# Graph-network kernel: the gather streams wait one group further back, and each gets a limit on how far it runs ahead

## The chip, the cores and the metric

One core of a Trainium2 chip runs the whole program. The metric is the device time of one execution in microseconds (us); less is better. TensorE, VectorE (DVE), ScalarE (ACT) and GpSimd (POOL) compute; SyncE (SP) and POOL's own queue start transfers. A row gather or row scatter is an indirect DMA and is started by GpSimd.

## The reference, cut to what matters

100,000 nodes with 16 features, 50,000 edges (`src`, `dst`, an 8-way type, a 90-way type, a weight, 16 attributes). Four graph layers follow each other, each on `h = relu(layernorm(x))` and added back to `x`:

```python
x = x + L0(h)   # two graph attention layers (3 heads x 32, then 1 x 32), SELU, linear
x = x + L1(h)   # two relational convolutions, 8 relations, mean over edges of one relation
x = x + L2(h)   # msg = w * xi * xj / (5 + 0.9*xi + 0.1*xj), summed at the source node
x = x + L3(h)   # per-edge 16x16 matrix out of 90, times an attention scalar, summed at dst
```

Each layer needs `table[src[e]]` for every edge e, a sum (or a softmax) over the edges of one destination, and then dense work per node.

## The kernel before, in words

The edges are first sorted by destination. Slot (p, s) holds one edge, p a partition and s a column, with T = 392 columns. An edge's source row lies in an HBM table, so one column of 128 edges is one indirect DMA from GpSimd (a "gather"): `ring[:, s]` receives the 128 rows. A "stream" is the loop over the 392 columns in one stage. Between the stages stands a barrier of all engines and every stage has its own semaphores.

The stages in order, with the line of their gather or scatter:

- setup, counting and sorting (gather L521, scatter L809), then a stage in which 56 columns of the first attention stream are gathered (L984);
- **attention 1**: columns 56 to 391 (L1147). DVE takes them in 9 chunks of 48: `edge_score(i)` (first instruction L1271) waits until its columns have landed, `edge_sum(i)` and `edge_mix(i)` (last instruction L1362, semaphore `mix_ok`) follow. Between them dense work goes on (3 blocks for a chunk);
- **attention 2**: 392 columns (L1487), chunks of 40: `edge_score(i)` starts at L1617, `edge_sum(i)` raises `ring_free` at L1637. The ring holds 200 columns;
- **relational 1**: 392 columns (L1817); `expand` (L2010, semaphore `expand_ok`) takes 8 columns at a time, 49 times, and TensorE and ScalarE work on its result;
- **relational 2**: 392 columns (L2128), a ring of 240; TensorE transposes 4 columns at a time (L2160, `lift_ok`), DVE reduces the product (L2240, L2243) and then raises `taken`, 98 times;
- **source sums**: gathers (L2338) alternating with accumulating scatters (L2352); the pacing function serves only its first 80 gathers;
- a dense stage, in which GpSimd has nothing to do;
- **last layer**: 392 gathers (L2573); DVE takes 8 columns at a time: `choose` (L2643), then L2655 to L2665, `mats_used` after L2660. On the same GpSimd queue, behind the last gather, 393 scatters of the finished rows (L2583) follow, paced by `spaced`, which always waits for the group two back. One plain copy to the output ends the kernel.

GpSimd runs its queue in order. `paced` stands ahead of every gather of the five named streams. At each eighth column it waits until an earlier group of eight has wholly landed: below column 160 (`RUN`) the group two back, so that up to 16 gathers may be under way, and from column 160 on the group just started, so that GpSimd waits until nothing of its own is under way (a "drain" below). A full ring is kept from being overwritten by one `hold` per 40 columns (`hold` is a plain semaphore wait). In attention 1 and the last layer the ring has all 392 columns and there is no such wait.

Of the kernel before, what the change touches and what calls it, by code (L numbers as in the profile page):

```python
# [49 lines left out]
def hold(engine, sem, value):  # L50

    engine.wait_ge(sem, value)


BATCH = 8


RUN = 160


def paced(engine, landing, s, first=0):

    n = s // BATCH - (1 if s >= RUN else 2)
    if s % BATCH == 0 and n >= first // BATCH:
        engine.wait_ge(landing[n], 16 * BATCH)


def spaced(engine, landing, s):  # L70


    n = s // BATCH - 2
    if n >= 0:
        engine.wait_ge(landing[n], 16 * BATCH)


def all_landed(engine, landing, lo, hi):

    for n in range(lo // BATCH, -(-hi // BATCH)):  # L80
        engine.wait_ge(landing[n], 16 * (min(hi, BATCH * (n + 1)) - BATCH * n))
# [6 lines left out]
def gnn_kernel(nc, x, src, dst, edge_attr_16, edge_type_8, edge_type_90, edge_weight,  # L88
# [45 lines left out]
    with ExitStack() as top:  # L134
# [43 lines left out]
        with ExitStack() as ctx:  # L178
            def tmp(name, shape, dt=F32):
                return sb(name, shape, dt, ctx)  # L180

            def sem(name):
                return semaphore(ctx, name)
# [753 lines left out]
        with ExitStack() as ctx:  # L937
# [29 lines left out]
            with nc.Block() as block:  # L967
# [9 lines left out]
                @block.gpsimd  # L977
                def _(pool):
                    nc.gpsimd.iota(trash[:], pattern=[[1, T + 1]], base=NP, channel_multiplier=T + 1,
                                   allow_small_or_imprecise_dtypes=True).then_inc(trash_ok, 1)  # L980
                    hold(pool, src_ok, 1)
                    for s in range(EARLY):
                        paced(pool, gat_in, s)
                        pool.indirect_dma_start(ring1[:, s, :], None, t_gat1,  # L984
                                                bass.IndirectOffsetOnAxis(src_i[:, s:s + 1], 0)
                                                ).then_inc(gat_in[s // BATCH], 16)
                    all_landed(pool, gat_in, 0, EARLY)
# [101 lines left out]
        with ExitStack() as ctx:  # L1089
# [3 lines left out]
            def sem(name):  # L1093
# [3 lines left out]
            NE, EW = 9, 48  # L1097
# [27 lines left out]
            step_s, arg_ok, exp_e, mix_ok, tail_ok, bm_ok, reach_ok, at_ok, att_ok, ext_ok = (sem(n) for n in (  # L1125
                "step", "arg", "exp_e", "mix", "tail", "bm", "reach", "at", "att", "ext"))
# [15 lines left out]
            with nc.Block() as block:  # L1142
                @block.gpsimd
                def _(pool):
                    for s in range(EARLY, T):
                        paced(pool, gat_in, s, EARLY)
                        pool.indirect_dma_start(ring1[:, s, :], None, t_gat1,  # L1147
                                                bass.IndirectOffsetOnAxis(src_i[:, s:s + 1], 0)
                                                ).then_inc(gat_in[s // BATCH], 16)
                    all_landed(pool, gat_in, EARLY, T)  # L1150
# [255 lines left out]
        QN = 40  # L1406
# [14 lines left out]
        with ExitStack() as ctx:  # L1421
# [3 lines left out]
            def sem(name):  # L1425
# [3 lines left out]
            NR = 5  # L1429
# [3 lines left out]
            lead = tmp("lead", [P, 1])  # L1433
# [26 lines left out]
            mix_ok, elu_ok, ready_ok, flip_ok, copy_ok, prod_ok, var_ok, root_ok, row_ok = (  # L1460
                sem(n) for n in ("mix", "elu", "ready", "flip", "copy", "prod", "var", "root", "row"))
            x_in = [sem(f"x_in{k}") for k in range(4)]
            ring_free, const_ok = sem("ring_free"), sem("const")
# [16 lines left out]
            with nc.Block() as block:  # L1480
                @block.gpsimd
                def _(pool):
                    for s in range(T):
                        if s % QN == 0 and s >= NR * QN:
                            hold(pool, ring_free, s // QN - NR + 1)
                        paced(pool, gat_in, s)
                        pool.indirect_dma_start(ring[:, s % (NR * QN), :], None, t_gat2,  # L1487
                                                bass.IndirectOffsetOnAxis(idx2[:, s:s + 1], 0)
                                                ).then_inc(gat_in[s // BATCH], 16)
                    all_landed(pool, gat_in, 0, T)  # L1490
# [271 lines left out]
        def relation_pass(tag, table, table_out, F, CW, weights, root, bias, NR, norm, setup):  # L1762

            EXPAND = NREL * F // P
            ES = 8
            BS = 4 // EXPAND
            NB = ES // BS
            subs = [w // ES for w in widths]
            first = [sum(subs[:i]) for i in range(NE)]
            sub_at = {}  # L1770
            for i in range(NE):
                for s in range(subs[i]):
                    n = 3 * i - 1 + (s + 1) // 2
                    sub_at.setdefault(max(n, 0), []).append((i, s))
            PROD = 1024 if CW * QN > 1024 else 1536
            with ExitStack() as ctx:
# [3 lines left out]
                def sem(name):  # L1780
                    return semaphore(ctx, f"{tag}_{name}")
# [21 lines left out]
                step_s, expand_ok, lift_ok, drop_ok, turn_ok, y_in, sum_ok, tail_ok, ext_ok = (  # L1803
                    sem(n) for n in ("step", "expand", "lift", "drop", "turn", "y_in", "sum", "tail", "ext"))
# [4 lines left out]
                with nc.Block() as block:  # L1809
                    @block.gpsimd  # L1810
                    def _(pool):
                        for s in range(T):
                            if s % QN == 0 and s >= NR * QN:
                                i = s // QN - NR
                                hold(pool, expand_ok, first[i] + subs[i])
                            paced(pool, gat_in, s)
                            pool.indirect_dma_start(ring[:, s % (NR * QN), :], None, table,  # L1817
                                                    bass.IndirectOffsetOnAxis(idx2[:, s:s + 1], 0)
                                                    ).then_inc(gat_in[s // BATCH], 16)
                        all_landed(pool, gat_in, 0, T)  # L1820
# [265 lines left out]
        with ExitStack() as ctx:  # L2086
# [6 lines left out]
            F, CW, NR = CH, FEAT, 6  # L2093
            ES = 4
            subs = [w // ES for w in widths]
            first = [sum(subs[:i]) for i in range(NE)]
            sub_at = {}
            for i in range(NE):
# [17 lines left out]
            step_s, lift_ok, drop_ok, product_ok, taken, tail_ok, ext_ok = (  # L2116
                sem(n) for n in ("step", "lift", "drop", "product", "taken", "tail", "ext"))
            flip_ok, copy_ok, prod_ok, used_ok, var_ok, root_ok, row_ok = (
                sem(n) for n in ("flip", "copy", "prod", "used", "var", "root", "row"))
            with nc.Block() as block:  # L2120
                @block.gpsimd
                def _(pool):
                    for s in range(T):
                        if s % QN == 0 and s >= NR * QN:
                            i = s // QN - NR
                            hold(pool, lift_ok, first[i] + subs[i])
                        paced(pool, gat_in, s)
                        pool.indirect_dma_start(ring[:, s % (NR * QN), :], None, t_rel2,  # L2128
                                                bass.IndirectOffsetOnAxis(idx2[:, s:s + 1], 0)
                                                ).then_inc(gat_in[s // BATCH], 16)  # L2130
                    all_landed(pool, gat_in, 0, T)
# [164 lines left out]
        ES = 8  # L2296
# [4 lines left out]
        with ExitStack() as ctx:  # L2301
# [10 lines left out]
            lead = tmp("lead", [P, FEAT])  # L2312
# [226 lines left out]
        with ExitStack() as ctx:  # L2539
# [3 lines left out]
            def sem(name):  # L2543
                return semaphore(ctx, f"l3_{name}")

            subs = [w // ES for w in widths]
            first = [sum(subs[:i]) for i in range(NE)]
# [3 lines left out]
            lead = tmp("lead", [P, 1])  # L2551
# [12 lines left out]
            lead_ok, lead_in, pick_ok, mats_ok, mats_used, tail_ok, ext_ok, final_ok, step_s = (sem(n) for n in (  # L2564
                "lead", "lead_in", "pick", "mats", "mats_used", "tail", "ext", "final", "step"))
            dense_out, copied = sem("dense_out"), sem("copied")
            sent = [sem(f"sent{n}") for n in range(T // BATCH + 1)]
            with nc.Block() as block:  # L2568
                @block.gpsimd
                def _(pool):  # L2570
                    for s in range(T):
                        paced(pool, gat_in, s)
                        pool.indirect_dma_start(ring[:, s, :], None, t_last,  # L2573
                                                bass.IndirectOffsetOnAxis(idx2[:, s:s + 1], 0)
                                                ).then_inc(gat_in[s // BATCH], 16)
                    pool.wait_ge(dense_out, 16)
                    for s in range(T + 1):
                        if s % QN == 0 and s < T:
                            hold(pool, final_ok, s // QN + 1)
                        if s == T:  # L2580
                            hold(pool, final_ok, NE + 1)
                        spaced(pool, sent, s)
                        pool.indirect_dma_start(fin, bass.IndirectOffsetOnAxis(home_i[:, s:s + 1], 0),  # L2583
                                                X[:, s, :], None).then_inc(sent[s // BATCH], 16)
                    all_landed(pool, sent, 0, T + 1)
                    all_landed(pool, gat_in, 0, T)
# [120 lines left out]
```

## Time and profile before

| | |
|---|---|
| time, median of 3 runs | 6640.55 us (6635.97 to 6644.13) |
| profiled execution: span, first to last instruction | 6645.3 us |
| GpSimd busy | 4320.0 us (65%) |
| DVE busy | 3659.5 us (55%) |
| TensorE busy | 2965.9 us (45%) |
| ScalarE busy | 1167.0 us (18%) |
| granted TensorE clock, mean | 0.654 of full |
| HBM traffic | 53 GB/s over the span |

No engine is busy throughout. The stages have different limits, so the shares say little; what counts is, within a stage, which wait ends last. The time of an indirect DMA on POOL is the time in which GpSimd prepares it, not the transfer. The idle time "<-issue" is the short pause between two POOL instructions in which nothing is waited for; "<-DMA" is a wait for a transfer, "<-POOLq L132" the wait at the barrier between two stages.

### The profile page before, as it was taken

To read this page: it belongs to the slowest core of one execution; us is meant where nothing else is said; L and a number is where in the kernel's file an instruction comes from. 1 tells how busy PE (TensorE), PEld (TensorE's weight loads), DVE (VectorE), ACT (ScalarE), POOL (GpSimd) and SP (SyncE) were. 2 spreads that over 40 slices of the span, in tenths; PEclk is the share of its full clock that TensorE was granted. 3 is DMA by queue.
4 is the path that set the end of the run, shared out by engine and by line. 5 is a ranking of instruction groups with operands and counts; after the bars stand their busy time and mean duration, and the time that the engine had idled before them with its cause. 6 is when DMAs were issued, how large, how long until landed. Compare 5 with 4: busy or idle time off the path is not lost. (4 is left out here: it accounts for less than half of the span.)

```text
span 6645.3 us, 44822 instructions
## 1 busy us (share of the span) xinstructions
PE 2965.9 (45%) x13056; PEld 2260.1 (34%) x13056; DVE 3659.5 (55%) x8917; ACT 1167.0 (18%) x1912; POOL 4320.0 (65%) x3949
## 2 busy tenths in 40 slices
PE   5798699974444344447655443111111002544000
PEld 2477555543333233346644333111111001433000
DVE  8855499976555566654347667433322068876000
ACT  0265454532222233211111100000000000000000
POOL 4666555557762776376657665888888823766776
PEclk9899899985666555556667665555555555776555
DMA  2122222221110322123222212222222234211001
GB/s 41 22 62 70 56 67 67 66 66 12 20 17 14 89 60 65 47 64 100 84 87 60 64 53 72 52 36 36 44 27 27 5 96 154 57 50 37 7 7 44
DMA packets 283354, 350.11 MB, mean 53 GB/s; under 512 B 133518, under 2 KB 204432, under 8 KB 281970
## 3 DMA queue, kind: packets, MB, share of 16 engines
q1 hardware_dynamic: 112158, 295.24, 13.2%
q0 software_dynamic: 169376, 41.40, 7.8%
q10 hardware_dynamic: 1576, 10.60, 0.7%
q8 instruction: 105, 1.72, 0.1%
q14 instruction: 139, 1.14, 0.1%
HBM read 231.06 MB, written 122.29 MB: 53 GB/s over the span
## 5 line engine op out<-in xcount | busy, mean ns | idle before, releaser
L2352 POOL DMA_INDIRECT acc<-l_rows,l_uniq x392 | 624.1, 1592 | 121.0 <-issue 108.6
L2573 POOL DMA_INDIRECT l_ring<-t_last,idx x392 | 392.4, 1001 | 366.5 <-ACTq L2568 207.6
L521 POOL DMA_INDIRECT pay<-in_x,gidx x392 | 460.1, 1174 | 235.4 <-DMA pay<-in_x,gidx 114.3
L2393 PE MATMUL ps_l<-l_msg,l_alike 128*128 128x16 f32 x784 | 176.3, 376 | 962.4 <-DVE l_msg L2456 962.4
L1487 POOL DMA_INDIRECT g_ring<-t_gat,idx x392 | 416.1, 1062 | 278.7 <-issue 110.1
L1817 POOL DMA_INDIRECT r_ring<-t_rel,idx x392 | 414.6, 1058 | 254.6 <-issue 110.3
L809 POOL DMA_INDIRECT t_sort<-pay,c_pos x392 | 384.8, 982 | 296.3 <-DVE c_pos L875 196.3
L901 PE MATMUL ps_c<-plane,c_hit 128*128 128x400 f32 x1568 | 542.6, 499 | 1.2 <-ACT c_hit L827 1.2
L2128 POOL DMA_INDIRECT r_ring<-t_rel,idx x392 | 392.7, 1002 | 224.4 <-issue 110.4
L2338 POOL DMA_INDIRECT l_ring<-t_mix,idx x392 | 426.3, 1087 | 154.6 <-issue 119.1
L2393 PEld LDWEIGHTS ps_l<-l_msg,l_alike 128*128 128x128 f32 x784 | 171.0, 331 | 967.7 <-DVE l_msg L2456 967.7
L1147 POOL DMA_INDIRECT ring<-t_gat,src_i x336 | 368.5, 1097 | 151.5 <-issue 93.3
L2583 POOL DMA_INDIRECT fin<-X,home_i x393 | 376.9, 959 | 119.8 <-issue 119.8
L2614 PE MATMUL ps_l<-w_rel,l_pick 128*128 128x256 f32 x784 | 275.7, 528 | 272.7 <-DVE l_pick L2643 272.7
L901 PEld LDWEIGHTS ps_c<-plane,c_hit 128*128 128x128 f32 x1568 | 296.4, 190 | 208.3 <-ACT c_hit L827 1.6
L2614 PEld LDWEIGHTS ps_l<-w_rel,l_pick 128*128 128x128 f32 x784 | 212.0, 277 | 336.1 <-DVE l_pick L2643 291.6
L2451 DVE TENSOR_SCALAR l_den<-l_ring 128x128 f32<-128x128 f32 x49 | 11.2, 228 | 564.3 <-DMA l_ring<-t_mix,idx 564.3
L871 DVE SCALAR_TENSOR_TENSOR c_junk<-iota_lo,lo_f,ps_c 128x400 f32<-128x400 f16 x392 | 231.0, 623 | 63.1 <-PE ps_c L901 63.0
L688 PE MATMUL ps_a<-w_ext,a_act_t 96*128 96x128 f32 x1600 | 224.5, 286 | 40.4 <-DVE a_row L612 39.9
L688 PEld LDWEIGHTS ps_a<-w_ext,a_act_t 96*128 96x128 f32 x1600 | 214.8, 200 | 61.7 <-DVE a_row L612 49.8
L1520 PE MATMUL ps_g<-ident,g_ex 128*128 128x128 f32 x300 | 71.9, 426 | 327.0 <-DVE g_ex L1704 327.0
L622 DVE SCALAR_TENSOR_TENSOR a_act_t<-a_ex,a_pos 96x512 f32<-96x512 f32 x200 | 137.4, 687 | 143.5 <-ACT a_ex L729 140.1
(529 smaller groups left out, 8145.0 us busy)
## 6 DMA issues: line engine op xcount, KB each, us to landing
c_rows_d<-row_dst SPq DMA_DIRECT2D x98, 256.0 KB, 3.3
l_keys<-row_at SPq DMA_DIRECT2D x49, 512.0 KB, 4.2
l_typs<-row_typ SPq DMA_DIRECT2D x49, 512.0 KB, 3.7
g_hs<-t_gat SPq DMA_DIRECT2D x30, 660.0 KB, 4.7
acc<-r_zero SPq DMA_DIRECT2D x60, 320.0 KB
t_rel<-r_row SPq DMA_DIRECT2D x30, 640.0 KB, 3.5
r_hs<-t_rel SPq DMA_DIRECT2D x30, 640.0 KB, 4.7
d_gain<-acc SPq DMA_DIRECT2D x30, 640.0 KB, 6.0
```

Source lines behind the costliest of these rows:

```text
L521: pool.indirect_dma_start(pay[:, s, 8:PAY], None, x, bass.IndirectOffsetOnAxis(gidx[:, s:s + 1], 0)).then_inc(gat_in[s // BATCH], 16)
L688: last = mm(ps[:, at:at + WIDE], act_t[:, u, P * m:P * (m + 1)], w2_ext[:], start=True, stop=True, skip_group_check=True)
L809: pool.indirect_dma_start(t_sort, bass.IndirectOffsetOnAxis(pos[:, e:e + 1], 0), pay[:, e, :], None).then_inc(sent, 16)
L901: last = mm(ps[:, bank:bank + LO], hit[:, b, j, P * s:P * (s + 1)], plane[:, b, LO * j:LO * (j + 1)], start=(j == 0), stop=(j == 1))
L1487: pool.indirect_dma_start(ring[:, s % (NR * QN), :], None, t_gat2, bass.IndirectOffsetOnAxis(idx2[:, s:s + 1], 0)).then_inc(gat_in[s // BA ...
L1817: pool.indirect_dma_start(ring[:, s % (NR * QN), :], None, table, bass.IndirectOffsetOnAxis(idx2[:, s:s + 1], 0)).then_inc(gat_in[s // BAT ...
L2128: pool.indirect_dma_start(ring[:, s % (NR * QN), :], None, t_rel2, bass.IndirectOffsetOnAxis(idx2[:, s:s + 1], 0)).then_inc(gat_in[s // BA ...
L2338: pool.indirect_dma_start(ring[:, s, :], None, t_mix, bass.IndirectOffsetOnAxis(idx2[:, s:s + 1], 0)).then_inc(gat_in[s // BATCH], 16)
L2352: pool.indirect_dma_start(acc[r], bass.IndirectOffsetOnAxis(uniq[:, s:s + 1], 0), rows[:, (s // ES) % RR, s % ES, :], None, compute_op=ALU.add
L2573: pool.indirect_dma_start(ring[:, s, :], None, t_last, bass.IndirectOffsetOnAxis(idx2[:, s:s + 1], 0)).then_inc(gat_in[s // BATCH], 16)
L2583: pool.indirect_dma_start(fin, bass.IndirectOffsetOnAxis(home_i[:, s:s + 1], 0), X[:, s, :], None).then_inc(sent[s // BATCH], 16)
L2614: last = mm(ps[:, at:at + 256], pick[:, e % 2, s], w_rel[:].rearrange("p i o -> p (i o)"), start=True, stop=True)
```

## The change

It has two parts. `paced` loses its special case: at every eighth column, over the whole stream, it waits for the group two back (the gathers 9 to 16 back). And a new wait, `credit`, is put ahead of it in the five streams: at every eighth column beyond `lead`, the consumer's semaphore must have reached (s - lead) / per, rounded up, so that no column more than `lead` beyond those used is asked for (and the seven behind it). The lead is 96 columns in attention 1, 64 in attention 2 and relational 1, 32 in relational 2, 40 in the last layer. It replaces the three ring holds. In the diff the middle stream of `relation_pass` is relational 1. The stage that starts the first 56 columns and the 80 early gathers of the source sums call `paced` only below column 160.

```diff
-RUN = 160
 def paced(engine, landing, s, first=0):
-    n = s // BATCH - (1 if s >= RUN else 2)
+    n = s // BATCH - 2
     if s % BATCH == 0 and n >= first // BATCH:
         engine.wait_ge(landing[n], 16 * BATCH)
+def credit(engine, used, s, lead, per):
+    if s % BATCH == 0 and s > lead:
+        engine.wait_ge(used, -(-(s - lead) // per))
@@ attention 1
                     for s in range(EARLY, T):
+                        credit(pool, mix_ok, s, 2 * EW, EW)
                         paced(pool, gat_in, s, EARLY)
@@ attention 2
-                        if s % QN == 0 and s >= NR * QN:
-                            hold(pool, ring_free, s // QN - NR + 1)
+                        credit(pool, ring_free, s, 64, QN)
                         paced(pool, gat_in, s)
@@ relational 1
-                            if s % QN == 0 and s >= NR * QN:
-                                i = s // QN - NR
-                                hold(pool, expand_ok, first[i] + subs[i])
+                            credit(pool, expand_ok, s, 64, ES)
                             paced(pool, gat_in, s)
@@ relational 2
-                        if s % QN == 0 and s >= NR * QN:
-                            i = s // QN - NR
-                            hold(pool, lift_ok, first[i] + subs[i])
+                        credit(pool, taken, s, 32, ES)
                         paced(pool, gat_in, s)
@@ last layer
                     for s in range(T):
+                        credit(pool, mats_used, s, 40, ES)
                         paced(pool, gat_in, s)
```

## Rows read from the trace of the kernel before

**Rows 1.** Page, costliest groups: the scatters that end the kernel.

```profile
L2583 POOL DMA_INDIRECT fin<-X,home_i x393 | 376.9, 959 | 119.8 <-issue 119.8
```

**Rows 2.** Timeline of POOL, attention 2: the gather of column 168.

```profile
2402.17 1.08 POOL L1487 DMA_INDIRECT g_ring<-t_gat,idx  x1 [1.63 <-DMA g_ring<-t_gat,idx]
```

**Rows 3.** Windows of L1147, L1487, L2128, L2573: length, busy (count), clock, DMA, GB/s.

```profile
1545.15:1692.70 147.55, 114.68 (x104) 0.62 0.12 17
1692.70:2057.50 364.80, 253.86 (x232) 0.61 0.11 18
...
2166.70:2388.00 221.30, 169.08 (x160) 0.50 0.35 83
2388.00:2752.30 364.30, 247.04 (x232) 0.50 0.25 60
...
3455.70:3665.00 209.30, 160.41 (x160) 0.68 0.24 65
3665.00:4038.50 373.50, 232.25 (x232) 0.67 0.21 55
...
5572.10:5779.00 206.90, 157.15 (x160) 0.73 0.31 94
5779.00:6123.50 344.50, 235.24 (x232) 0.72 0.18 47
```

**Rows 4.** Waits of POOL: us in total, times, longest.

```profile
POOL r_ring L2128 <- DMA r_ring<-t_rel,idx: 71.3, 25, 4.5
...
POOL g_ring L1487 <- DMA g_ring<-t_gat,idx: 59.3, 30, 3.7
...
POOL ring L1147 <- DMA ring<-t_gat,src_i: 50.4, 29, 2.8
POOL l_ring L2573 <- DMA l_ring<-t_last,idx: 48.9, 30, 1.8
...
POOL r_ring L2128 <- PE r_ps L2160: 8.5, 4, 2.2
```

**Rows 5.** Timeline of DVE: starts of chunks in attention 1 and 2.

```profile
1896.21 0.21 DVE L1271 CAST idx<-ring 128x48 int32<-128x48 f32 x1 [11.67 <-DMA ring<-t_gat,src_i]
...
1972.59 0.21 DVE L1271 CAST idx<-ring 128x48 int32<-128x48 f32 x1 [13.86 <-DMA ring<-t_gat,src_i]
...
2390.39 0.22 DVE L1617 TENSOR_TENSOR g_score<-g_ring,g_ad_slot 128x40 f32<-128x40 f32 x1 [3.57 <-DMA g_ring<-t_gat,idx]
...
2513.96 0.22 DVE L1617 TENSOR_TENSOR g_score<-g_ring,g_ad_slot 128x40 f32<-128x40 f32 x1 [11.09 <-DMA g_ring<-t_gat,idx]
...
2577.57 0.22 DVE L1617 TENSOR_TENSOR g_score<-g_ring,g_ad_slot 128x40 f32<-128x40 f32 x1 [11.52 <-DMA g_ring<-t_gat,idx]
...
2753.66 0.21 DVE L1617 TENSOR_TENSOR g_score<-g_ring,g_ad_slot 128x32 f32<-128x32 f32 x1 [0.61 <-DMA g_ring<-t_gat,idx]
```

**Rows 6.** Timeline of DVE, relational 1: expand steps 15, 30, 37, 39, 42 and 48.

```profile
3041.98 1.22 DVE L2010 TENSOR_TENSOR r_msg<-r_ring,r_hot 128x1024 f32<-128x1024 f32 x1
...
3202.41 1.29 DVE L2010 TENSOR_TENSOR r_msg<-r_ring,r_hot 128x1024 f32<-128x1024 f32 x1
...
3286.33 1.23 DVE L2010 TENSOR_TENSOR r_msg<-r_ring,r_hot 128x1024 f32<-128x1024 f32 x1 [7.39 <-DMA r_ring<-t_rel,idx]
...
3310.59 1.23 DVE L2010 TENSOR_TENSOR r_msg<-r_ring,r_hot 128x1024 f32<-128x1024 f32 x1 [9.66 <-DMA r_ring<-t_rel,idx]
...
3347.92 1.23 DVE L2010 TENSOR_TENSOR r_msg<-r_ring,r_hot 128x1024 f32<-128x1024 f32 x1 [7.23 <-DMA r_ring<-t_rel,idx]
...
3424.28 1.22 DVE L2010 TENSOR_TENSOR r_msg<-r_ring,r_hot 128x1024 f32<-128x1024 f32 x1
```

**Rows 7.** Relational 2: the fourth reduce of DVE; the gather of column 48.

```profile
3489.91 1.01 DVE L2243 TENSOR_REDUCE r_Y<-r_chosen 128x64 f32<-128x512 f32 x1
...
3515.74 1.27 POOL L2128 DMA_INDIRECT r_ring<-t_rel,idx  x1 [0.30 <-issue]
```

**Rows 8.** The line L1487: its transfers, from issue to landing.

```profile
DMA to landing us min/median/max: 2.3/2.4/14.6
```

## The prediction

> **What bounds the kernel now.** I read the timeline of GpSimd first, then the windows of each gather line, then the waits of the engine that takes the gathered columns, last the places where the new waits would stand.
>
> A gather costs GpSimd about 0.94 us when nothing disturbs it, and the pause to the next is 0.30 us. A wait that is already satisfied adds nothing: the 393 closing scatters carry a wait "two groups back" at every column, and their whole idle time is the ordinary pause, 119.8 / 393 = 0.305 us [rows 1]. A drain does cost: the gather of column 168 starts after 1.63 us of idle [rows 2], 1.33 us more than the pause. There are 29 drains in each of five streams (columns 160, 168, ..., 384).
>
> The windows show it as a rate. In relational 2 the first 160 columns took 209.3 us, 1.308 us each, the other 232 took 373.5 us, 1.610 each; the work inside the gathers per column stayed the same, 160.41 / 160 = 1.003 and 232.25 / 232 = 1.001 us. In attention 2 it is 1.383 against 1.570, in the last layer 1.293 against 1.485, in attention 1 1.419 against 1.572 [rows 3]. So the tail of each stream is slower by its waits only.
>
> Do the stages wait for the streams? In attention 1 DVE stands 11.67 and 13.86 us at two neighbouring chunks, in attention 2 11.09 and 11.52 us [rows 5]; in relational 2 the gather-bound pace holds throughout; in the last layer the gathers and the closing scatters are one queue, so every microsecond of the stream is one of the kernel. Relational 1 is different: its DVE steps 15 to 30 run without any gather wait, and only the later ones meet it [rows 6].
>
> **Part one, the drains go.** What a stream saves is its waits for its own transfers less the pause that stays. Two estimates for each: (a) the waits minus 29 x 0.30 = 8.7 us, (b) the rate below column 160 put on the other 232 columns.
>
> - Attention 1: (a) 50.4 - 8.7 = 41.7 us [rows 4]; the last chunk DVE waits for ends at column 383, so 28 of 29 drains count: 40.3. (b) 232 x 1.419 = 329.2 against 364.8 us, 35.6, of which 34.4 [rows 3]. I take 38. Does DVE have room? The chunk from 1896.21 to 1972.59 us took 76.4 us with 13.9 of waiting [rows 5], so it needs 62.5 us; it holds six drains, 8.6 us, and the stream will ask 68. The stream stays the limit.
> - Attention 2: 59.3 us of waits [rows 4], of which one of 3.7 us lies near the start, far below column 160, and stays: 55.6 - 8.7 = 46.9. The last chunk waits only 0.61 us for its columns [rows 5], so I count the 25 drains up to column 359: 40.4 (a). (b) 232 x 1.383 = 320.9 against 364.3 is 43.4, times 25/29 is 37.4. I take 39. Room: 63.6 - 11.5 = 52.1 us of need per chunk [rows 5] against a stream that asks 40 x 1.383 = 55.3.
> - Relational 1: here DVE, with TensorE and ScalarE in its loop, becomes the limit. From step 15 (3041.98) to step 30 (3202.41) three rounds of five steps took 160.43 us, 53.5 a round, or 1.34 a column [rows 6]. From step 30 another 3.6 rounds put step 48 at 3202.4 + 192.5 = 3394.9, where it stood at 3424.28: 29 us saved. The stream must stay ahead of that. At step 30 DVE found its columns landed although 11 drains lay behind; without them the stream is at least 11 x 1.33 = 14.6 us further, and at some 1.38 us a column it loses 0.04 x 144 = 6 us of that up to step 48. I take 29; from below nothing, from above 61, if each of the 3.6 rounds shrank to the 44.7 us that it needs without waits (worked out under the rivals).
> - Relational 2: (a) 71.3 + 8.5 - 8.7 = 71.1 us; the four waits put down to TensorE are at ring holds, where a drain stands too, and the ring has been free for long, so they count as drains [rows 4]. (b) 232 x 1.308 = 303.5 against 373.5, 70.0 [rows 3]. I take 70.
> - Last layer: (a) 48.9 less one wait near the start of about 1.2, less 8.7, 39.0. (b) 232 x 1.293 = 300.0 against 344.5, 44.5. I take 41. It shifts the scatters whole: they need only DVE's chunks, the last of them long before its turn.
>
> Sum: 38 + 39 + 29 + 70 + 41 = 217 us. The lower estimates give 34.4 + 37.4 + 29 + 70.0 + 39.0 = 210, the upper ones 40.3 + 40.4 + 29 + 71.1 + 44.5 = 225. Nothing is late next: behind the last gather in each stage comes the same work of DVE, moved forward. The source sums, the sorting and the setup gather are not touched, since `paced` is called there only below column 160 or not at all.
>
> What may grow is the disturbance of a gather by DVE: in attention 2 a gather takes 1.06 us in the mean instead of 0.94, in both windows (169.08 / 160 and 247.04 / 232) [rows 3]. DVE's work per chunk is the same after the change, so I leave these 0.12 us per gather as they are. The Trainium skill, SBUF — State Buffer, Who interferes with whom, says that DVE's two-port modes and GpSimd take one shared port pair exclusively and that the later one is blocked for a whole instruction; read as "a stream at work for 78% instead of 68% of the time is blocked that much more often", it would add an estimated 0.12 x 10/68 = 0.018 us to each of 5 x 232 gathers, 21 us, and give 196 instead of 217. The equal means below and from column 160 speak against that reading.
>
> **Part two, the credits.** Each is one more wait at about 40 columns of a stream, free when satisfied [rows 1]. Is it satisfied? I compared, for each eighth column, the start of the gather with the consumer's step that the credit asks for. The tightest of all is in relational 2: column 48 needs four reductions; the fourth ended at 3489.91 + 1.01 = 3490.92, the gather started at 3515.74 [rows 7], 24.8 us later. This lies in the part that already runs at the new pace, so it is a margin of the new kernel too. All others are wider. The three ring holds that go were free as well. Cost: nothing; if the consumer fell 25 us behind, the stream would be held by as much as it lagged beyond that, and would have to catch up.
>
> **The rivals.**
>
> *The next wait comes up (partial gain).* In relational 1 a round of 61.6 us (3286.33 to 3347.92) held 9.66 + 7.23 = 16.9 us of gather wait [rows 6], so 44.7 of need; yet without gather waits it took 53.5. Waits for TensorE and ScalarE came up, 8.8 us a round. If the two attention stages did that too, attention 1 would need 62.5 + 8.8 = 71.3 of its 76.4 us per chunk and save 5.1 in 4.7 chunks, 24 us; attention 2 60.9 of 63.6, five times 2.7, 13 us. For relational 2, of whose need I show no row, I put half, 35 us. The last layer keeps its 41, since its scatters wait for the stream alone. With the 29 of relational 1: 142 us, 6499. Against it: in attention 2 a chunk before column 160 ran at the fast pace and DVE still waited 3.57 us for gathers [rows 5].
>
> *More (relational 1 gives all its drains).* 217 + 32 = 249 us: 6392. It needs the round to shrink to 44.7 us; its first half says no.
>
> *Slower: from column 160 on the drain keeps the store of started transfers from filling.* GpSimd would then go at the pace of landings instead of its own. At the median landing of 2.4 us [rows 8] one stream's tail takes 232 x 2.4 = 557 us instead of some 362 (the mean of the four in [rows 3]), and five of them make +975: about 7615. It decides once a gather costs over 1.56 us in the mean. Against it: 160 gathers under the same rule in each stream, and 393 scatters in a row without one wait [rows 1]. The Trainium skill, Perfetto Trace Analysis, DMA Instruction — SWDGE (GPSIMD), speaks of more descriptors being generated than fit the buffer; no row here shows such a stop.
>
> *The change does nothing.* Only if the consumers set every pace. The rates of [rows 3] rule it out but for other hidden couplings.
>
> **How the numbers follow.** Forecast 0.75, partial gain 0.12, more 0.05, nothing 0.03, slower 0.05. The span of 6645.3 us becomes about 6428; the profiled execution is 4.7 us above the median of the runs, so I take the sum from 6640.55 and predict 6424 us. The forecast's own range is 6410 to 6445. With the partial gain and the larger one the range is 6390 to 6500. Within 0.2% (13 us, about what a measurement of this kernel can tell from no change) nothing but the fourth rival falls. Faster 0.92, same 0.03, slower 0.05.
>
> **What the profile would show.** Right: no "<-DMA" idle on POOL from column 160 on, windows of 232 columns at 1.30 to 1.42 us each, five shorter stages (38, 39, 29, 70, 41 us), the source sums unchanged, no POOL wait for DVE in the five streams. Wrong: POOL waits that name DVE (a credit binds), gather durations above 1.1 us in the mean, or DVE waits for ScalarE and TensorE in place of those for the gathers.

## The result, and the profile after

| | before | changed |
|---|---|---|
| median, us | 6642.34 (6635.97 to 6650.12, 4 runs) | 6441.76 (6438.15 to 6455.07, 4 runs) |
| span of the profiled execution, us | 6645.3 | 6440.3 |

The ratio is 0.9705, 95% interval 0.9691 to 0.9719: 2.95% faster, 200.6 us. Forecast were 6424 us and 217 us less; the measured time lies inside the stated range of 6390 to 6500 and inside the forecast's own range of 6410 to 6445.

The windows of the gather lines in the changed kernel (length, POOL busy and count, granted clock, DMA share, GB/s), for attention 1, attention 2, relational 1, relational 2 and the last layer, first the part below column 160, then the 232 columns from it (of relational 1 only these):

```profile
1547.20:1693.70 146.50, 114.91 (x104) 0.62 0.12 17
1693.70:2025.10 331.40, 260.77 (x232) 0.62 0.12 20
...
2135.10:2355.70 220.60, 169.01 (x160) 0.50 0.36 83
2355.70:2679.00 323.30, 252.53 (x232) 0.50 0.27 67
...
2977.20:3288.20 311.00, 240.28 (x232) 0.63 0.35 101
...
3361.50:3570.70 209.20, 160.62 (x160) 0.66 0.24 65
3570.70:3876.90 306.20, 235.53 (x232) 0.72 0.25 68
...
5410.10:5616.90 206.80, 157.30 (x160) 0.71 0.32 94
5616.90:5918.90 302.00, 231.33 (x232) 0.75 0.21 54
```

The first parts are as they were. The second parts, 364.8, 364.3, 373.5 and 344.5 us in [rows 3], are now 331.4, 323.3, 306.2 and 302.0: both parts of a stream run at nearly one rate (a column takes 1.409 and 1.428 us in attention 1, 1.308 and 1.320 in relational 2). The busy time of the gathers is not quite what it was: 260.77 us instead of 253.86 in attention 1, 252.53 instead of 247.04 in attention 2, 235.53 instead of 232.25 in relational 2, 231.33 instead of 235.24 in the last layer. In relational 1 it fell as well, from 249.75 us in the kernel before to 240.28:

```profile
3044.50:3421.50 377.00, 249.75 (x232) 0.61 0.30 91
```

How these changes bear on the forecast is said further down.

The waits of POOL in the changed kernel (us in total, times, longest):

```profile
POOL l_ring L2575 <- DMA l_ring<-t_last,idx: 13.4, 41, 1.2
...
POOL ring L1153 <- DMA ring<-t_gat,src_i: 10.7, 35, 0.3
POOL g_ring L1492 <- DMA g_ring<-t_gat,idx: 10.6, 25, 3.3
POOL r_ring L2129 <- DMA r_ring<-t_rel,idx: 9.5, 31, 0.3
POOL r_ring L1820 <- DMA r_ring<-t_rel,idx: 8.2, 27, 0.3
...
POOL r_ring L1820 <- DVE r_msg L2013: 0.3, 1, 0.3
```

A mean of 0.3 us per "wait" is only the ordinary pause: the semaphore was there. Of the 48.9 to 79.8 us in [rows 4] nothing is left but one stall of 3.3 us near the start of attention 2 and one of 1.2 in the last layer, which were there before. The first shows what a wait two groups back can still cost: column 24 waits for columns 8 to 15, and the gather of column 15 took 14.2 us to land, where the median of the line is 2.5. In the five streams only one wait names DVE, of 0.3 us: the credits are never waited for.

DVE at neighbouring chunk starts of attention 2, to be held against [rows 5]:

```profile
2469.65 0.22 DVE L1622 TENSOR_TENSOR g_score<-g_ring,g_ad_slot 128x40 f32<-128x40 f32 x1 [3.54 <-DMA g_ring<-t_gat,idx]
...
2525.49 0.22 DVE L1622 TENSOR_TENSOR g_score<-g_ring,g_ad_slot 128x40 f32<-128x40 f32 x1 [3.90 <-DMA g_ring<-t_gat,idx]
```

55.84 us instead of 63.61, with 3.9 us of waiting instead of 11.5: the stream is still the limit, by a little. And DVE in relational 1, steps 15, 30 and 48, for [rows 6]:

```profile
2977.40 1.28 DVE L2013 TENSOR_TENSOR r_msg<-r_ring,r_hot 128x1024 f32<-128x1024 f32 x1
...
3136.58 1.29 DVE L2013 TENSOR_TENSOR r_msg<-r_ring,r_hot 128x1024 f32<-128x1024 f32 x1
...
3328.81 1.23 DVE L2013 TENSOR_TENSOR r_msg<-r_ring,r_hot 128x1024 f32<-128x1024 f32 x1
```

No gather wait is left; step 48 stands 192.2 us after step 30 (192.5 forecast).

Stage lengths, from the start of a stage's first gather or scatter to that of the next stage, in us, by the profiles of all kernels of this study ("sources" has the dense stage behind them in it; a change of 0.1 us is rounding):

| kernel | setup | att. 1 | att. 2 | rel. 1 | rel. 2 | sources | last | span |
|---|---|---|---|---|---|---|---|---|
| before | 720.6 | 621.5 | 661.7 | 627.4 | 618.2 | 1498.1 | 551.6 | 6645.3 |
| changed | 723.5 | 587.9 | 628.1 | 598.2 | 551.2 | 1497.5 | 508.9 | 6440.3 |
| drains gone, no credits | 727.6 | 589.0 | 628.1 | 598.3 | 553.9 | 1496.0 | 505.8 | 6443.2 |
| credits only | 724.6 | 633.9 | 670.0 | 625.0 | 633.9 | 1497.0 | 552.8 | 6681.6 |
| near leads | 733.0 | 587.9 | 628.2 | 598.1 | 550.9 | 1497.8 | 503.5 | 6443.5 |
| short leads | 723.4 | 624.9 | 734.2 | 598.3 | 657.3 | 1497.4 | 763.2 | 6942.9 |
| waits everywhere | 721.7 | 586.3 | 629.0 | 597.9 | 552.5 | 1497.5 | 506.5 | 6436.5 |
| drain by four | 725.7 | 705.4 | 788.4 | 728.8 | 724.8 | 1525.7 | 660.3 | 7220.7 |
| first stream too | 676.2 | 587.8 | 632.3 | 598.0 | 551.2 | 1495.2 | 506.1 | 6392.4 |
| credit one earlier | 721.1 | 621.9 | 652.0 | 619.7 | 615.4 | 1496.3 | 552.9 | 6625.4 |
| drain first | 732.5 | 622.0 | 652.6 | 621.9 | 608.6 | 1496.0 | 553.5 | 6632.3 |
| credit twice | 720.9 | 635.3 | 673.0 | 628.7 | 636.1 | 1496.3 | 553.6 | 6689.9 |

(Sorting takes 677 us in each, the closing scatters with the copy 521 to 524, the stage of the first 56 columns 82, with drains by four 98.) The setup stage moves by several us from run to run without any edit: 720.6 to 733.0. The last column is the span of one profiled execution.

### The profile page after: what moved, and what is told of

Read it like the earlier page. It is cut to its first block and busy times, and to the rows that moved or that the text cites. A ratio compares the mean times of both kernels' runs of the same rounds, so it can differ in the third digit from the quotient of the medians.

```text
span 6440.3 us, 45016 instructions
## 1 busy us (share of the span) xinstructions
PE 2945.9 (46%) x13056; PEld 2248.0 (35%) x13056; DVE 3659.0 (57%) x8917; ACT 1167.9 (18%) x1912; POOL 4324.5 (67%) x3949
## 5 line engine op out<-in xcount | busy, mean ns | idle before, releaser
L526 POOL DMA_INDIRECT pay<-in_x,gidx x392 | 459.6, 1172 | 237.1 <-DMA pay<-in_x,gidx 108.3
L2406 ACT COPY l_rows<-ps_l 128x128 f32<-128x128 f32 x49 | 13.0, 266 | 1141.5 <-PE ps_l L2394 1141.5
```

Of the source, the lines that this page charges most:

```text
L526: pool.indirect_dma_start(pay[:, s, 8:PAY], None, x, bass.IndirectOffsetOnAxis(gidx[:, s:s + 1], 0)).then_inc(gat_in[s // BATCH], 16)
```

## The experiments

My theory: the drains are the whole gain and the credits nothing. The rivals: the credits give or take a part; the gain is more or less than the drains' idle time because something else moves with them.

### Each part alone

The drains taken out of the kernel before, ring holds kept, no credits:

```diff
-    n = s // BATCH - (1 if s >= RUN else 2)
+    n = s // BATCH - 2
```

> Part one of the change alone: the wait is for the group two back everywhere, the three ring holds stay, no credit is added. If the drains are the whole gain, this is the changed kernel again: about 6441 us (within 0.2%), with the same stage lengths (587.9, 628.1, 598.2, 551.2, 508.9 us). If the credits give part of it (by keeping early gathers out of the way of other transfers), this one is slower than 6441 by that part, seen in relational 1, whose stream would now run furthest ahead.

Measured: 6437.7 us median, ratio to before 0.969 (0.9674 to 0.9706), against 0.9703 (0.9685 to 0.972) for the changed kernel run again on the same day. But for the setup stage the lengths are those of the changed kernel within 3.1 us. Part one is the whole gain, as far as runs that differ by 8 us in the median can tell.

The credits alone, with the drains kept:

```diff
 (changed kernel)
-    n = s // BATCH - 2
+    n = s // BATCH - (1 if s >= 160 else 2)
```

> Part two alone: the credits stand, the drains from column 160 on stay. If the credits are free and do nothing: 6642 us, within 0.2%, and no wait of GpSimd that names DVE. If they hold streams back: over 6655; if they help: below 6629.

Measured: 6684.41 us median, ratio 1.0064 (1.0046 to 1.0083). That is 43 us slower than before. It lies in the branch "over 6655", but not for the reason given there: no stream was held back. The step that a credit asks for was done at least 24.7 us before each gather. Nine rows do name DVE (11.4 us in attention 2, 9.0 in attention 1), all of them at drains, where the landing was the wait that ended last. The first timeline row is a drain of attention 2 in this kernel (gather of column 200), the second a drain of the kernel without any credit ahead of it, one group earlier than the third, which had a ring hold ahead of it; both of the latter are of the kernel before.

```profile
2469.44 0.96 POOL L1492 DMA_INDIRECT g_ring<-t_gat,idx  x1 [2.22 <-DMA g_ring<-t_gat,idx]
```

```profile
2439.47 0.94 POOL L1487 DMA_INDIRECT g_ring<-t_gat,idx  x1 [1.75 <-DMA g_ring<-t_gat,idx]
...
2451.54 0.94 POOL L1487 DMA_INDIRECT g_ring<-t_gat,idx  x1 [2.21 <-DMA g_ring<-t_gat,idx]
```

A drain idles about 1.7 us by itself and 2.2 us when a second, satisfied wait stands ahead of it in the source. In attention 1 the median over the 29 drains went from 1.67 to 2.18, in the last layer from 1.64 to 2.14. The ring holds of the kernel before had paid this price already, at five drains in attention 2 and four in relational 2, so "the three ring holds that go were free as well" was wrong by about half a microsecond at each. The longer idle explains the stages: the growth of the mean idle per drain times 29, plus the change of the gathers' busy time (which fell), gives +13 us in attention 1 (measured +12.4), +9 in attention 2 (+8.3), +14 in relational 2 (+15.7), +1 in the last layer (+1.2).

### Where the credits would bind

Two kernels with shorter leads, all else as in the changed kernel:

```diff
-credit(pool, mix_ok, s, 2 * EW, EW)     # near: 80   short: 64
-credit(pool, ring_free, s, 64, QN)      # near: 48   short: 32
-credit(pool, expand_ok, s, 64, ES)      # near: 48   short: 32
-credit(pool, taken, s, 32, ES)          # near: 16   short: 8
-credit(pool, mats_used, s, 40, ES)      # near: 16   short: 0
```

> The changed kernel with shorter leads, chosen by the margins in its trace (margin = time from the consumer's step to the gather that asks for it; a column of lead is worth 1.31 to 1.41 us): attention 1 lead 80 instead of 96 (smallest margin 30.4 becomes 30.4 - 16 x 1.41 = 8 us), attention 2 48 instead of 64 (29.1 becomes 7), relational 1 48 instead of 64 (26.4 becomes 5), relational 2 16 instead of 32 (24.9 becomes 4), last layer 16 instead of 40 (32.9 becomes 2). My theory: every credit is still satisfied when it is read, no wait names DVE for more than a few us in total, time 6441 within 0.2%. The rival, that a credit costs something beyond its margin (a late increment, a slower start after it), gives one or more stages over 5 us longer.

Measured: 6445.28 us (one run), stage lengths as in the changed kernel within 1 us but for the setup stage and the last layer (5 us shorter); waits for DVE 0.3 us at most. The margins read from the trace are real: leads cut down until, by the working above, 2 to 8 us of margin are left cost nothing that is seen.

> The changed kernel with leads that must bind: attention 1 64, attention 2 32, relational 1 32, relational 2 8, last layer 0. By the margins: attention 1 falls short by 35.7 - 32 x 1.41 = -9.4 us at each of 7 chunks, stage +66 us; attention 2 by 29.1 - 32 x 1.38 = -15 us at each of 9 chunks, +135 us; relational 2 about even at the typical column (10.5 us of lead against 10 to 17 of lag), +20 to +100 us; last layer by the lag of 5.5 us at each of 48 groups, +265 us or more; relational 1 shows waits for DVE up to 16 us, but its stage is set by DVE's loop, which still has 24 columns in hand, so its length stays within 10 us of 598. Rival: relational 1 also grows by its waits, since its stream is a limit too.

Measured: 6944.61 us (one run). The waits of POOL:

```profile
POOL l_ring L2575 <- DVEq L2665: 282.8, 48, 19.4
...
POOL g_ring L1492 <- DVE g_S L1642: 128.9, 9, 15.8
POOL r_ring L2129 <- DVEq L2246: 114.9, 20, 5.9
...
POOL ring L1153 <- DVE g_mix L1368: 77.0, 7, 17.1
...
POOL r_ring L1820 <- DVE r_msg L2013: 12.7, 2, 12.4
```

Attention 2: 15.3 to 15.8 us at 8 of 9 chunks, as forecast (15), and +106 us of stage (135 forecast). Last layer: 5.6 us at the typical group (5.5 forecast), +254 us (265). Attention 1: +37 us (66 forecast) with seven waits of 77 us together; the total over gathers from column 160 on of what they take over 0.94 us fell from 42 to 18 us at the same time. Relational 2: +106, a little above the range. Relational 1: +0.1 us with 12.7 us of waiting, nearly all of it one wait of 12.4 us at column 40, so that wait cost nothing; the rival (the stage grows by its waits) is out for it, and no other wait stood in this stream to try it on.

### Is a satisfied wait free?

```diff
 def paced(engine, landing, s, first=0):
     n = s // BATCH - 2
-    if s % BATCH == 0 and n >= first // BATCH:
+    if n >= first // BATCH:
         engine.wait_ge(landing[n], 16 * BATCH)
 def credit(engine, used, s, lead, per):
-    if s % BATCH == 0 and s > lead:
+    s -= s % BATCH
+    if s > lead:
         engine.wait_ge(used, -(-(s - lead) // per))
```

> The changed kernel, with both waits of the eighth column repeated at all eight columns of a group: seven times two more waits for each group, about 3,000 in all, all of them already satisfied. If a satisfied wait is free on GpSimd: the same 6441 us and the same pause of 0.30 us. If each costs even 0.05 us: +150 us.

Measured: 6438.2 us (one run), and the pause stays 0.30 us at every column. The compiled program has 46,437 instructions instead of 45,016, 1,421 more, so one wait of each pair became an instruction of its own, seven times at each of 203 groups. They are free where nothing on that queue has to be waited for.

What makes the half microsecond ahead of a drain? Three variants of the kernel with the credits alone:

```diff
 (1) def credit: the credit of column s stands ahead of gather s - 1
+    s += 1
     if s % BATCH == 0 and s > lead:
 (2) the order of the two waits
-    credit(pool, ring_free, s, 64, QN)
     paced(pool, gat_in, s)
+    credit(pool, ring_free, s, 64, QN)
 (3) in credit, twice
         engine.wait_ge(used, -(-(s - lead) // per))
+        engine.wait_ge(used, -(-(s - lead) // per))
```

> Drains and credits as in the run with the credits alone (6684 us), but each credit stands one column earlier on the queue, ahead of the gather before the drain. There a drain with a credit ahead of it idled 2.2 us instead of 1.67. If that half microsecond is the satisfied wait itself, bare because GpSimd has nothing else to do there, it now hides under the gather: idle back to 1.67, time about 6642. If the credits cost something else (their number, or the streams held back), the time stays near 6684.

> The run with the credits alone, with the two waits of a column in the other order: first the wait for the landing, then the satisfied credit. Theory: the satisfied wait now comes after the drain and is bare, idle 2.2 us, about 6684 us. If the order matters, so that only the first of two costs: 1.67 and 6642.

> The run with the credits alone, with every credit issued twice. If each bare wait ahead of a drain costs the half microsecond, the drains idle 2.7 us and the four streams that set their stages grow by 4 x 29 x 0.5 = 58 us more, some 6735 us. If the cost comes once however many waits there are: 2.2 us and 6684.

Measured: (1) 6627.08 us, (2) 6634.3, (3) 6691.93, one run each, with the kernel before at 6644.61 beside them. The same drain (column 168 of attention 2) in the three kernels:

```profile
2398.36 1.03 POOL L1493 DMA_INDIRECT g_ring<-t_gat,idx  x1 [1.67 <-DMA g_ring<-t_gat,idx]
```

```profile
2412.80 1.03 POOL L1492 DMA_INDIRECT g_ring<-t_gat,idx  x1 [1.69 <-DMA g_ring<-t_gat,idx]
```

```profile
2415.74 0.95 POOL L1493 DMA_INDIRECT g_ring<-t_gat,idx  x1 [2.23 <-DVE g_S L1643]
```

In (1) and (2) the idle is back at 1.67 and 1.69 us. For (2) this was not expected, so the half microsecond is not the bare time of a satisfied wait that comes last.

What the order changes can be read from the trace. Where two waits stand ahead of one gather, the compiled program gives one of them to the gather and makes the other an instruction of its own in front of it, 203 in all. In the kernel with the credits alone it is the landing wait (L66, the line in `paced`), in (2) it is the credit (L80). The first row is the one that belongs to column 168 of attention 2 in the kernel with the credits alone, the second the one of the same column in (2):

```profile
L66 POOLq EVENT_SEMAPHORE  x1: 17/17/17, 2417.2 to 2417.2; - x1
```

```profile
L80 POOLq EVENT_SEMAPHORE  x1: 17/17/17, 2404.0 to 2404.0; - x1
```

The first comes at 2417.2 us and its gather starts at 2417.91, 0.7 us later; the second comes at 2404.0, 8.8 us before its gather (2412.80), which carries the landing wait itself. It is so throughout. At the 145 drains of the kernel with the credits alone the gather starts 0.70 us after the separate landing wait in the median (at most 1.0), at the nine drains with a ring hold in the kernel before 0.70 to 0.71 us after it; in (2) every credit comes 8 us or more ahead of its gather. In (1) the two waits stand ahead of different gathers; the program has 44,813 instructions, 203 fewer, and the credit is no instruction of its own. So (1) does not show that a credit "hides under the gather". The half microsecond goes with a landing wait that is an instruction of its own, not with the satisfied wait beside it. Why a gather starts later after such an instruction than with the wait on itself stays open.

(3) tells nothing more: its program has 45,016 instructions, as the one with single credits, so the doubled wait was merged away. It is also seen here how little a row's releaser says when two waits stand ahead of one gather: (3)'s drain is put down to DVE, although the step that it asks for was done long before.

(1) and (2) came 15 and 8 us under the 6642 expected. Most of that is in attention 2 (652.0 and 652.6 us where the kernel before has 661.7): with drains at the same 29 columns its gathers took 7 us less than the 247.04 before. In (1):

```profile
2384.90:2737.10 352.20, 240.02 (x232) 0.50 0.25 63
```

### More drains

```diff
-    n = s // BATCH - 2
-    if s % BATCH == 0 and n >= first // BATCH:
-        engine.wait_ge(landing[n], 16 * BATCH)
+    if s % BATCH == 0 and s // BATCH - 1 >= first // BATCH:
+        engine.wait_ge(landing[s // BATCH - 1], 16 * BATCH)
+    if s % BATCH == BATCH // 2:
+        engine.wait_ge(landing[s // BATCH], 16 * (BATCH // 2))
```

> The changed kernel with drains put back, at every fourth column and over the whole stream. By what a drain cost before (1.43 us in attention 1, 1.6 in attention 2, 2.4 in relational 2, 1.35 in the last layer) the stages grow by about 115, 145, 235 and 132 us; relational 1 becomes bound by its stream and grows by about 160, together some 7,230 us. On the stretched gathers of attention 1 from column 160 on (35.3 us in total over the undisturbed 0.94 us with drains by eight, 42.4 without): if a denser stream meets DVE more often, they fall to about 28 us; if they go with DVE's work alone, they stay at 35 to 42.

Measured: 7222.72 us (one run; 7,230 expected). The stages grew by 117.5, 160.3, 173.6 and 151.4 us where 115, 145, 235 and 132 were expected, relational 1 by 130.6 (160 expected). That the sum fits better than its parts is luck: the five stages grew by 733 us and not by 787, and another 45 came from two stages that the expectation left out, the first 56 columns and the early gathers of the source sums. The drain at a middle column, without a credit, idled about 1.7 us in the median, the one with a credit ahead 2.1 to 2.3. Relational 2's dear drains (a mean of 2.75 us before) stayed dear at the eighth columns (a mean of 2.78), while those at its middle columns idled 1.67 in the median; what makes them dear is not shown. The stretched gathers of attention 1 came to 32 us (250.44 less 232 x 0.94), between the 28 and the 35 of the two theories, so this one number decides for neither.

The windows from column 160 on in attention 1, attention 2 and relational 2:

```profile
1748.60:2165.10 416.50, 250.44 (x232) 0.60 0.10 16
...
2564.10:2983.10 419.00, 236.85 (x232) 0.50 0.22 53
...
4063.10:4477.10 414.00, 229.97 (x232) 0.66 0.19 52
```

The busy time of the same 232 gathers is 250.44, 253.86 and 260.77 us in attention 1 with drains by four, by eight and none; 236.85, 247.04, 252.53 in attention 2; 229.97, 232.25, 235.53 in relational 2. In each of these three, fewer drains come with longer gathers. In the other two the order fails. Relational 1 has 240.37, 249.75 and 240.28. The last layer has 235.24 with drains by eight in the kernel before and 231.33 without; there the kernel with the credits alone, also drained by eight but with its drains half a microsecond longer, had gathers 13.6 us shorter than before. And attention 2 had 240 us instead of 247 in (1) and (2) above, with as many drains. So it is not the density alone: with the same number of drains the sum moved by 7.0 us, when they went by 5.5. Where a gather falls beside DVE's work can count for much. In attention 1 of the changed kernel:

```profile
1701.14 3.15 DVE L1312 COPY_PREDICATED g_kept<-head_mask,g_S 128x2592 f32<-128x2592 uint32 x1
1701.36 3.72 POOL L1153 DMA_INDIRECT ring<-t_gat,src_i  x1 [0.30 <-issue]
```

A gather of 0.94 us that starts just after this instruction of DVE takes 3.72. No run here moves the place of the gathers by itself.

### The stream that was left

The setup gather (L521 before, L526 in the changed kernel) has drains of its own, which neither kernel touched:

```diff
-    if s >= BATCH and s % BATCH == 0:
-        pool.wait_ge(gat_in[s // BATCH - 1], 16 * BATCH)
+    paced(pool, gat_in, s)
```

> The changed kernel with the drains taken out of the setup gather too (L521 before), where GpSimd waits 108 us at 39 drains. If that stream sets the end of its stage: about 50 us less (39 drains x 1.3 us). My theory: the stream there is tied to the consumer by its own holds and the dense work ends the stage, so the time is that of the changed kernel within 5 us.

> The changed kernel itself, beside the others on one chip: 6441 us within 0.2%.

Measured: 6398.05 us (6394.37 to 6399.65), ratio to before 0.9631 (0.9613 to 0.9648); the changed kernel beside it 6445.63 us (6443.42 to 6448.98), ratio 0.9703 (0.9685 to 0.972). 47.6 us less: my theory fell, the stream did set the end of its stage. The waits of DVE at the barrier that opens sorting, with the changed kernel run again first and the kernel with the setup drains gone second:

```profile
778.24 0.29 DVE L854 TENSOR_SCALAR c_hi<-iota_hi,h_f 128x256 f16<-128x256 f16 x1 [55.64 <-PEq L137]
```

```profile
726.29 0.29 DVE L853 TENSOR_SCALAR c_hi<-iota_hi,h_f 128x256 f16<-128x256 f16 x1 [3.52 <-PEq L137]
```

In the first DVE was done at 722.6 us and stood 55.6 us at the barrier. The row names TensorE's queue, but what it waited for was GpSimd, as the second shows. Without the drains the stream's last gather starts at 699.5 us instead of 765.2, the dense work ends the stage, and DVE waits 3.5 us. This is the fastest version measured.

## Why the prediction was right, by its own steps

**The drains are the cost, and a satisfied wait is none.** Right for the drains. The first experiment gives the whole gain by that line alone. "A wait that is already satisfied adds nothing" holds for the new kernel (1,421 more of them changed nothing). Beside a drain it can cost 0.5 us, by making the landing wait an instruction of its own; nine ring holds of the kernel before did that, and "free as well" was wrong for them.

**Attention 1, 38 us:** measured 33.6. **Attention 2, 39 us:** 33.6. **Relational 2, 70 us:** 67.0. **Last layer, 41 us:** 42.7. The term that was mis-sized is the one I set to nothing, the disturbance of the gathers ("I leave these 0.12 us per gather as they are"). Estimate (a), the drains' own idle time, less the growth of the busy time in the windows gives 40.3 - 6.9 = 33.4, 40.4 - 5.5 = 34.9, 71.1 - 3.3 = 67.8 and 39.0 + 3.9 = 42.9: each within 1.3 us of the stage. The net of the four is 11.8 us; the forecast's terms for them, 188 us, were 11.1 us above the 176.9 measured. Between the two profiled spans lie 205.0 us and between the medians 200.6, against 217.

The rule of the Trainium skill, SBUF — State Buffer, Who interferes with whom, read as "a denser stream is blocked more often", had given 21 us less than the sum, about 4.2 us more for the gathers of each stream. The traces have that sign in three streams of five, with 6.9, 5.5 and 3.3 us; in the last layer and relational 1 the gathers took 3.9 and 9.5 us less. So the reading comes near the forecast's error by size, but it is not borne out as a rule of density. The traces do not tell in which port mode DVE's instructions ran, so what the page says of the ports is not tested here. The equal means below and from column 160 that I held against the reading were no test: these two parts of a stream differ in more than the drains.

**Relational 1, 29 us:** 29.2. DVE waits for no gather in it any more, and in the kernel with short leads a wait of GpSimd of 12.4 us left the stage where it was. A stage's gain read from its own undisturbed rounds was better than one read from waits; its waits in the kernel before, less the 8.7 us of pause, come to 59.4 us, twice as much:

```profile
POOL r_ring L1817 <- DMA r_ring<-t_rel,idx: 68.1, 29, 5.3
```

**The credits, nothing:** right, with the smallest margin at 24.9 us, at columns 40 and 48 of relational 2 (24.8 us at column 48 before the change). They are free only because the drains went with them: beside the drains they cost 43 us.

**The rivals.** Partial gain: no; in attention 2 DVE still waits 3.5 to 3.9 us a chunk for gathers. More: no, relational 1 stayed at 53.1 to 53.4 us a round. Slower, by transfers piling up: no, not in 232 more columns of five streams. Nothing: no.

**What I had not read.** The setup stream was outside the change, so I passed over the 108 to 114 us that GpSimd waits there. The barrier wait of DVE behind it, in the kernel before, was the sign to follow up:

```profile
773.03 0.29 DVE L849 TENSOR_SCALAR c_hi<-iota_hi,h_f 128x256 f16<-128x256 f16 x1 [49.85 <-PEq L132]
```

## What to carry to other kernels

Where a queue waits for everything of its own to be back before it goes on, it pays the way of the last transfer each time: here 1.67 us of idle, with 2.4 us from issue to landing [rows 8] and 0.94 us of gather. Waiting for the group before that one cost nothing here, where eight gathers take 10 us and more, but for the one transfer of 14.2 us. The worth of such a drain is its idle time less the pause, less what the moved gathers lose (or gain) beside the other engines' work, and only in stages whose end it sets: look at who waits at the next barrier. A limit on running ahead can be sized from the trace, as the time from the consumer's step to the request that needs it; it costs nothing until that margin is used up.

## What the hardware showed that I had not expected

- Two waits ahead of one gather are not free at a drain. When the landing wait became an instruction of its own, the gather started 0.7 us after it and GpSimd's idle was about 2.2 us; with the landing wait on the gather itself it was 1.67 to 1.69. Which of the two is separated changed with their order in the source. What the 0.7 us are is not known.
- GpSimd gets through separate waits early where none of them blocks: each credit of (2) was worked off at least 8 us before its gather.
- The same 232 gathers take a different time depending on how they fall beside DVE's work: in attention 2 236.85 us with drains by four, 247.04 and 240.02 with drains by eight, 252.53 with none. A gather of 0.94 us took 3.72 beside one instruction of DVE.
